# Expert products one stage deeper on 64x64 quarters, down weights fetched by number, and a reordered start of the second attention layer

## The chip, the core and the metric

The kernel runs on one core of one Trainium2 chip. A core has a matrix engine (PE, with its weight loads shown apart as PEld), a vector engine (DVE), an activation engine (ACT), a general engine (POOL, GpSimd), a queue engine that here only starts transfers (SP), and 16 DMA engines that carry the transfers of all of them. The metric is the device time of one run of the whole program, in microseconds (us). Everything is computed in float32 except a few counting steps.

## The reference, cut to what matters

Two layers over 1024 tokens (8 tiles of 128) with 256 channels. Each layer adds a mixing step and a feed-forward step to x, each behind a layer norm and scaled by tanh of a gate. The change touches the feed-forward step of layer 0 and the mixing step of layer 1.

```python
# layer 0: x += tanh(g) * wkv(ln(x), ctx)     a decaying scan
# layer 0, feed-forward: 64 experts, 4 chosen for each token, plus shared experts
logits = flat @ router_w
scores = softmax(logits)
_, topk_idx = top_k(logits + router_bias, 4)
topk_scores = take_along_axis(scores, topk_idx); topk_scores /= topk_scores.sum()
g = silu(einsum('nd,edf->nef', flat, wg))       # wg, wu: 64 x 256 x 64
u = einsum('nd,edf->nef', flat, wu)
routed = einsum('ne,nef,efd->nd', comb, g * u, wd)   # wd: 64 x 64 x 256
# layer 1: x += tanh(g) * attention(ln(x), ctx)   16 heads of 16; a query tile sees the 128 keys of its own row
# layer 1, feed-forward on block-quantised (fp8-like) weights and activations
```

The kernel does not compute all 64 experts for all tokens. It sorts the (token, expert) picks into blocks of 64 rows that share an expert and computes each block with its expert's weights alone.

## The kernel before

**Blocks and pairs.** There are room for 128 blocks of S = 64 rows. Two blocks (j = 0, 1) stand side by side in the 128 rows of a group, two groups (b = 0, 1) make a pair, so a pair is 4 blocks and 256 rows, and there are NP = 32 pairs. In the first NPS = 16 pairs block i belongs to expert i, known when the program is built. The blocks of the last 16 pairs take the overflow; their experts are found at run time and stand in the row `eid_row`, from which an engine loads them into registers (`experts_of`, a TENSOR_LOAD and one register operation for each use).

**The work on one pair** n passes through all engines:

- POOL gathers the rows of the pair from DRAM into one of four buffers `xg` (L519, two indirect transfers), up to three pairs ahead.
- PE transposes them (helper L1118, 4 transposes, semaphore `xgT_ps`), ACT copies them from PSUM into `xgT` (L700).
- PE multiplies with the up weights (`wg` and `wu` of the expert side by side). In the first 16 pairs (L1263) a block's product has 64 columns of weights' output rows, so the two blocks j use two 64-wide halves of the array; in the last 16 (L1270) the product is 128x128 and the rows that belong to the other block are zero. Semaphore `gu`.
- ACT takes the silu of the gate half (L694, `sgb`), DVE multiplies it with the other half (L1003, `hb`).
- PE transposes `hb` (L1118, 2 transposes, `hT_ps`), ACT copies it into `hbT` (L705).
- PE multiplies with the down weights `moe_dn`, which hold all 64 experts in partitions 0 to 63 of `arena_dn`: 64 rows by 64 outputs for the first 16 pairs (L1291), 64 rows by 128 outputs, accumulated over j with the other block's columns zero, for the last 16 (L1294). Semaphore `mo_y`.
- ACT copies the result into `ysb` (L711, two buffers), SP stores it to `ys_dram` (L395), 256 KB a pair, semaphores `ys_out0` and `ys_out1`.

Each float32 product or transposed product shows as two passes in the trace where it has a separate weight load for each (16 records for the 8 up products of a pair, 8 for the 4 down products).

**The order on the engines** is written out by hand, as one step k of a loop per engine. PE's step k: up products of pair k, transposes of pair k+1, down products of pair k-1, transposes of `hb` of pair k. ACT's step k: silu k, `xgT` k+1, `hbT` k, `ysb` k-1. DVE's step: `hb` k, and then halves of the quantising of a weight matrix for the last stage (`weight_half`, 48 halves in all, 4 instructions each, L989 to L997); how many have been done after step n is told by `weight_halves(n)`. POOL finishes each weight (L511, `weight_rescale`) between its gathers.

**The end of the loop.** SP waits for the last up products, then starts six loads of keys and values of attention (`kva_load`, L384 and L385, 256 KB each, tiles 0 to 2), and then the last store L395. POOL, which has to wait for all stores, then gathers each token's four expert results (`gather`, L543, four indirect transfers a tile) for DVE to add (L1016, `combine`). PE in that time transposes the quantised weights (`mx_turns`, out of `mx_w`).

**The start of the attention.** For a tile: layer norm (DVE L1069 and L1071 statistics, POOL L444 and L447 inverse root, DVE L1049 `xnE`), transposes, ACT copy L744, query projection L1347, bias L1021 on DVE, square on ACT L740, inverse root on POOL L552 (`query_rms`), norm on DVE L1026, transposes, copy L1033 to `qT`, scores L1333, DVE maximum L1043 over them, then the transposed scores L1380, exponentials on ACT (L753), and the product with the values L1341. POOL's layer-norm step for tile 1 stands behind all four gathers of tile 2; PE computes the scores of tile 0 in its step k = 1.

## Time and profile before

| | us |
|---|---|
| median of the three runs | 546.87 |
| lowest, highest | 544.39, 546.98 |
| the profiled execution | 548.21 |
| its span, first to last instruction | 546.5 |
| mean granted clock of TensorE, share of full | 0.863 |
| PE busy | 419.4 (77%) |
| DVE busy | 355.8 (65%) |
| POOL busy | 240.2 (44%) |
| ACT busy | 161.9 (30%) |

The profile is of one execution. Its page sums up busy time by engine, and cuts the span into 40 equal slices with a digit in tenths for each engine, for the granted clock (PEclk) and for the DMA engines. The chain of work that ended last is followed back from the last instruction, at each step to what released it. The timeline lists instructions with start, length and, in brackets, the idle time ahead of them and who ended it. Ends of matmuls are modelled, so the start of whoever waits for a product is the safer sign of when it was ready. The expert loop runs from 182 us to 309 us, the attention layer from 309 us to about 420 us, the last feed-forward stage from there to the end.

### The profile page before, as it was taken

The numbers are of one execution on the slowest core, as the hardware profiler recorded it, in microseconds if no ns is written. First come the engines' busy times: TensorE is split into PE (matmuls) and PEld (weight loads), VectorE is DVE, ScalarE is ACT, GpSimd is POOL, SyncE is SP. The second block draws the span as 40 slices with busy tenths as digits, with TensorE's granted clock in tenths as the row PEclk, the third lists the DMA queues.
The fourth block names the chain that finished last, engine by engine and source line by source line (L and its number), as shares of the span: only waits on it lengthen the run. The fifth ranks groups of instructions, "written<-read, shape, count | busy, mean of one in ns | idle before, by whom it ended". The sixth has DMA issues, their size and how long they took to land.

```text
span 546.5 us, 8075 instructions
## 1 busy us (share of the span) xinstructions
PE 419.4 (77%) x2711; PEld 287.4 (53%) x2711; DVE 355.8 (65%) x898; ACT 161.9 (30%) x374; POOL 240.2 (44%) x336
## 2 busy tenths in 40 slices
PE   0777653389685699999999934788988599999885
PEld 0565532234264465578888623566665245555543
DVE  3658889993644014567877425577851599999992
ACT  1444520123100155543333430344442122222210
POOL 2355533323203667766561156756200345555451
PEclk9999855579869599999999875599995599999997
DMA  7126999900055656554652422243200000000000
GB/s 213 35 71 214 284 276 220 231 14 1 1 118 153 229 163 173 163 148 102 124 113 80 150 83 68 69 133 100 79 1 1 1 1 11 10 11 10 10 10 20
DMA packets 66968, 53.19 MB, mean 97 GB/s; under 512 B 37872, under 2 KB 59504, under 8 KB 66928
## 3 DMA queue, kind: packets, MB, share of 16 engines
q1 hardware_dynamic: 56688, 34.09, 24.4%
q0 software_dynamic: 4608, 12.59, 9.5%
q10 hardware_dynamic: 5632, 6.00, 3.2%
q8 instruction: 23, 0.38, 0.3%
q14 instruction: 17, 0.14, 0.1%
HBM read 37.98 MB, written 14.68 MB: 96 GB/s over the span
## 4 chain that ended last, share of the span: by engine, by line
PE 44%; DVE 23%; issue 15%; POOL 10%; ACT 4%; DMA 4%; another core or an unknown queue 0%; POOLq 0%; SPq 0%; DVEq 0%; ACTq 0%
PE psum L1118 8%; PE psum L1212 5%; PE psum L1270 5%; PE psum L1294 5%; PE psum L1263 5%; POOL arena_dn L588 3%; PE psum L1235 3%; POOL mx_w L591 2%; DVE arena_dn L828 2%; PE psum L1380 2%; PE psum L1333 2%; PE psum L1386 2%; DMA x_res<-in_x_dram 1%; DVE arena_dn L935 1%; POOL arena_up L543 1%
## 5 line engine op out<-in xcount | busy, mean ns | idle before, releaser
L519 POOL DMA_INDIRECT shared<-h_dram,tok_u x64 | 63.9, 998 | 60.0 <-PE psum L1235 28.0
L1407 PE MATMUL psum<-arena_dn 128*128 128x512 f32 x128 | 59.7, 621 | 3.7 <-ACT arena_dn L762 3.7
L1118 PE MATMUL psum<-ident,arena_dn 128*128 128x128 f32 x112 | 23.2, 334 | 49.0 <-DVE arena_dn L858 15.0
L1118 PEld LDWEIGHTS psum<-ident,arena_dn 128*128 128x128 f32 x112 | 15.5, 169 | 56.1 <-issue 23.3
L1407 PEld LDWEIGHTS psum<-arena_dn 128*128 128x128 f32 x128 | 24.6, 198 | 34.2 <-issue 28.4
L1003 DVE TENSOR_TENSOR h1T<-psum,h1T 128x128 f32<-128x128 f32 x32 | 9.3, 291 | 50.4 <-ACT h1T L694 41.8
L588 POOL TENSOR_TENSOR arena_dn<-arena_dn 128x512 f32<-128x512 f32 x16 | 20.3, 1270 | 45.7 <-DVE arena_dn L974 45.7
L1118 PE MATMUL psum<-ident,arena_up 128*128 128x128 f32 x128 | 23.6, 312 | 21.5 <-DVE arena_up L1049 13.5
L543 POOL DMA_INDIRECT arena_up<-ys_dram,slot_u x32 | 31.5, 985 | 16.3 <-issue 16.3
L1118 PE MATMUL psum<-ident,mx_w 128*128 128x128 f32 x128 | 23.4, 320 | 12.7 <-POOL mx_w L591 9.6
L1294 PE MATMUL psum<-arena_dn,h1T 64*128 x128 | 31.9, 389 | 0.5 <-ACT h1T L705 0.5
L1118 PEld LDWEIGHTS psum<-ident,arena_up 128*128 128x128 f32 x128 | 16.1, 156 | 30.1 <-issue 9.8
L1423 PE MATMUL psum<-arena_dn,mx_w 128*128 128x256 f32 x128 | 30.7, 395 | 0.1
L1212 PE MATMUL psum<-h1T,shared 128*128 128x512 f32 x64 | 29.7, 623 | 0.0
L1118 PE MATMUL psum<-ident,shared 128*128 128x128 f32 x128 | 21.5, 294 | 9.3 <-DMA shared<-h_dram,tok_u 9.3
L1118 PEld LDWEIGHTS psum<-ident,mx_w 128*128 128x128 f32 x128 | 16.5, 161 | 22.5 <-POOL mx_w L591 11.7
L1423 PEld LDWEIGHTS psum<-arena_dn,mx_w 128*128 128x128 f32 x128 | 25.0, 200 | 3.7 <-ACT mx_w L773 0.4
L1294 PEld LDWEIGHTS psum<-arena_dn,h1T 64*128 64x128 f32 x128 | 22.7, 186 | 6.0 <-issue 3.1
L1016 DVE SCALAR_TENSOR_TENSOR x_res<-arena_up,combs,x_res 128x256 f32<-128x256 f32 x32 | 15.4, 481 | 15.2 <-DMA arena_up<-ys_dram,slot_u 14.6
L444 POOL TENSOR_SCALAR small<-mv 128x1 f32<-128x1 f32 (+2 forms) x26 | 6.4, 246 | 41.9 <-DVE mv L1085 20.0
L1043 DVE TENSOR_REDUCE arena_up<-psum 128x16 f32<-128x2048 f32 x8 | 18.3, 2293 | 7.7 <-PE psum L1333 5.9
L511 POOL TENSOR_TENSOR mx_w<-mx_w,wac 128x256 f32<-128x256 f32 x24 | 14.8, 620 | 19.1 <-DVE mx_w L997 18.3
(215 smaller groups left out, 993.0 us busy)
## 6 DMA issues: line engine op xcount, KB each, us to landing
ys_dram<-ysb SPq DMA_DIRECT2D x32, 256.0 KB
arena_up<-in_L_ffn_wg_dram SPq DMA_DIRECT2D x8, 512.0 KB, 7.5
arena_up<-in_L_ffn_wu_dram SPq DMA_DIRECT2D x8, 512.0 KB, 8.3
arena_dn<-in_L_ffn_wd_dram SPq DMA_DIRECT2D x4, 1024.0 KB, 11.6
va_dram<-mx_w ACTq DMA_DIRECT2D x8, 256.0 KB, 4.4
kT_dram<-mx_w ACTq DMA_DIRECT2D x8, 256.0 KB, 4.4
arena_up<-kT_dram SPq DMA_DIRECT2D x8, 256.0 KB, 2.7
arena_up<-va_dram SPq DMA_DIRECT2D x8, 256.0 KB, 3.0
```

The costliest lines, as they stand in the source:

```text
L519: pool.indirect_dma_start(out=xg[n % 4][:, b, :], out_offset=None, in_=h1_dram[:, :], in_offset=bass.IndirectOffsetOnAxis(ap=tok_u[:, 2 * ...
L543: pool.indirect_dma_start(out=yk[n % 3][k], out_offset=None, in_=ys_dram[:, :], in_offset=bass.IndirectOffsetOnAxis(ap=slot_u[:, n * K + k ...
L588: pool.tensor_tensor(haF[h], haF[h], heF[h], ALU.subtract).then_inc(sem("hint"), 1)
L1043: dve.tensor_reduce(qn[b % 2].rearrange("p (g j) d -> p j g d", g=4)[:, :, :, HD], psum[:, 0:4, :].rearrange("p j (g n) -> p j g n", g=4), ...
L1118: return pe.transpose(dst, src, ident[0:k, 0:k])
L1212: ins = pe.matmul(bank[2 * part + n % 2][:, :], sgu_w[:, c, part * SH + f * P:part * SH + (f + 1) * P], h1T[:, c, hf * 512:(hf + 1) * 512] ...
L1235: ins = pe.matmul(bank[2 + t % 2][:, 0:D], hs[:, f, t * P:(t + 1) * P], sd_w[:, f, :], start=(f == 0), stop=(f == 3))
L1263: ins = pe.matmul(bank[2 + k % 2][at, 2 * F * b:2 * F * (b + 1)], xgT[k % 2][:, b, c, j, at], moe_up[:, c, Q * (2 * k + b) + j, :], start= ...
L1270: ins = pe.matmul(bank[2 + k % 2][:, 2 * F * b:2 * F * (b + 1)], xgT[k % 2][:, b, c, j, :], moe_up[:, c, experts[k][Q * b + j], :].rearran ...
L1294: ins = pe.matmul(bank[6 + n % 2][:, b * D:(b + 1) * D], hbT[n % 2][0:F, b, j, :], moe_dn[:, experts[n][Q * b + j], :].rearrange("p a d -> ...
L1407: ins = pe.matmul(bank[2 + 2 * part + h][:, :], xTF[s][:, c, :], mx_gu[:, c, lo:lo + HW], start=(c == 0), stop=(c == C - 1))
L1423: ins = pe.matmul(bank[1][:, 0:D], hTF[s][:, k, :], mx_dn[:, k, :], start=(k == 0), stop=(k == 7))
```

## The change

Five edits:

1. **One stage deeper.** PE's step k is now: up k, transposes k+1, down k-2, `hb` transposes k-1. ACT's step: silu k, `xgT` k+1, `ysb` k-2, `hbT` k-1. The loops have one step more.
2. **Down weights by number, on quarters.** In the last 16 pairs SP loads the four experts' down weights of a pair from DRAM into a new double buffer `dnS`, experts j = 0 into partitions 0 to 63 and j = 1 into partitions 64 to 127; `hbT` puts its block j = 1 into partitions 64 to 127 as well (two ACT copies where there was one); and each down product is 64 rows by 64 outputs, on the quarter of the array that belongs to its rows and outputs. Nothing in `hbT` has to be zero now, so DVE's two clearing instructions go.
3. **Weight halves.** Nine halves in four steps in the last 16 pairs, where it was seven in three.
4. **Last store first.** SP's last store goes ahead of the loads of keys and values.
5. **Tile 0's attention first.** The scores of tile 0 and their maximum move one step earlier, the transposes of tile 2's row and their copy move behind tile 0's transposed scores and exponentials, and POOL's four gathers of tile 2 are split around `query_rms(0)` and the layer-norm step of tile 1.

```diff
-    return min(min(max(n - 4, 0), NPS - 5) + 7 * max(n - NPS + 1, 0) // 3, 2 * NWC)
+    return min(min(max(n - 4, 0), NPS - 5) + 9 * max(n - NPS + 1, 0) // 4, 2 * NWC)
...
+            def dn_load(n):
+                s = n % 2
+                if n >= NPS + 2:
+                    sp.wait_ge(sem("mo_y"), n - 1)
+                for x, v in enumerate(experts_of(mybir.EngineType.SP, n)):
+                    b, j = x // Q, x % Q
+                    sp.dma_start(dnS[s][j * F:(j + 1) * F, b, :], wd[bass.ds(v, 1)].rearrange("a f d -> f (a d)"))\
+                      .then_inc(sem(f"dn_in{s}"), 16)
+
+            sp.wait_ge(sem("eid"), 1)
             for n in range(NP):
-                if n == NP - 1:
-                    sp.wait_ge(sem("gu"), NG // 2)
-                    for b in range(2):
-                        sp.wait_ge(sem(f"kva_out{b}"), 32 * (T // 2))
-                    for t in range(3):
-                        kva_load(t)
+                if NPS <= n + 2 < NP:
+                    dn_load(n + 2)
                 sp.wait_ge(sem("ysb"), n + 1)
                 sp.dma_start(ys_dram[n * 2 * P:(n + 1) * 2 * P, :].rearrange("(b p) d -> p b d", p=P),
                              ysb[n % 2][:, :, :]).then_inc(sem(f"ys_out{n % 2}"), 16)
-            for n in range(3, T):
+            sp.wait_ge(sem("gu"), NG // 2)
+            for b in range(2):
+                sp.wait_ge(sem(f"kva_out{b}"), 32 * (T // 2))
+            for n in range(T):
                 kva_load(n)
...
+            def down(n):
+                pe.wait_ge(sem("hbT"), n + 1)
+                if n >= NPS:
+                    pe.wait_ge(sem(f"dn_in{n % 2}"), 64 * ((n - NPS) // 2 + 1))
+                reach(pe, sem("ysb"), n - 1)
...
+                            ins = pe.matmul(bank[6 + n % 2][at, b * D:(b + 1) * D], hbT[n % 2][j * F:(j + 1) * F, b, at],
+                                            dnS[n % 2][j * F:(j + 1) * F, b, :], start=True, stop=True)
...
-                                ins = pe.matmul(bank[6 + n % 2][:, b * D:(b + 1) * D], hbT[n % 2][0:F, b, j, :],
-                                                moe_dn[:, experts[n][Q * b + j], :].rearrange("p a d -> p (a d)"),
-                                                start=(j == 0), stop=(j == Q - 1))
...
+                    if n < NPS:
+                        act.copy(hbT[n % 2][0:F], turned).then_inc(sem("hbT"), 1)
+                    else:
+                        act.copy(hbT[n % 2][0:F, :, 0:S], turned[:, :, 0:S])
+                        act.copy(hbT[n % 2][F:2 * F, :, S:P], turned[:, :, S:P]).then_inc(sem("hbT"), 1)
...
+            gather(0, range(K))
+            gather(1, (0, 1))
+            row_rms(0)
+            gather(1, (2, 3))
+            gather(2, (0,))
+            query_rms(0)
+            gather(2, (1,))
+            row_rms(1)
+            gather(2, (2, 3))
...
+                if k == 0:
+                    score_max(0)
```

On PE, in a step of the last 16 pairs, the instructions between the up products of one pair and those of the next stood before as follows (`shared` is the gathered row buffer, `h1T` holds `hb` and `hbT`, `arena_dn` the down weights):

```order
L1118 MATMUL psum<-ident,shared 128x128 [waits xgT,xg0]
L1118 MATMUL psum<-ident,shared 128x128 x3
L1294 ISA [waits ysb,hbT]
L1294 MATMUL psum<-arena_dn,h1T 128x256
...
L1118 MATMUL psum<-ident,h1T 64x128 [waits hbT,hb]
L1118 MATMUL psum<-ident,h1T 64x128
L1249 TENSOR_LOAD eid_row [waits hb,xgT]
```

and stand now, on PE in the same place, as follows (the helper for transposes is L1153 now, and `h1T` holds `dnS` too):

```order
L1153 MATMUL psum<-ident,shared 128x128 [waits xgT,xg2]
L1153 MATMUL psum<-ident,shared 128x128 x3
L1311 MATMUL psum<-h1T 64x256 [waits ysb,dn_in1,hbT]
L1311 MATMUL psum<-h1T 64x256 x3
L1153 MATMUL psum<-ident,h1T 64x128 [waits hbT,hb]
L1153 MATMUL psum<-ident,h1T 64x128
L330 TENSOR_LOAD eid_row [waits hb,xgT]
```

The places are the same, but the down products now have 64 outputs and no register operation, wait for the fetched weights, and belong to the pair before the one they belonged to; the transposes behind them do too.

On SP, at the end of the expert loop, the stores of results and the loads of keys and values stood before as follows:

```order
L395 DMA ys_dram<-ysb 128x2x256 [waits ysb] x31
L384 DMA arena_up<-kT_dram 128x512 [waits kva_out1,kva_out0,gu]
L385 DMA arena_up<-va_dram 128x512
...
L395 DMA ys_dram<-ysb 128x2x256 [waits ysb]
L384 DMA arena_up<-kT_dram 128x512 [waits pv]
```

and now, on SP from the last fetch of down weights on (one of the four transfers of a fetch is shown):

```order
L330 TENSOR_LOAD eid_row [waits mo_y]
L401 ISA
L401 DMA h1T<-in_L_ffn_wd_dram 64x256
...
L409 DMA ys_dram<-ysb 128x2x256 [waits ysb] x3
L392 DMA arena_up<-kT_dram 128x512 [waits kva_out1,kva_out0,gu]
L393 DMA arena_up<-va_dram 128x512
```

The last store no longer stands behind six loads, and ahead of 16 of the stores stands a register load and four transfers.

On POOL, at the start of the attention, the gathers (L543) and the inverse roots (L444 with L447, and L552) stood before as follows:

```order
L543 DMA arena_up<-ys_dram,slot_u 128x256 x2
L552 TENSOR_TENSOR arena_up<-arena_up,mhalf 128x1 [waits ssq]
L543 DMA arena_up<-ys_dram,slot_u 128x256 x4
L444 TENSOR_SCALAR small<-mv 128x1 [waits mvE]
L447 TENSOR_TENSOR rstd<-small,mhalf 128x1 [waits isq]
L563 TENSOR_TENSOR x_res<-x_res,bias_bc 128x256 [waits xnE]
```

and now, on POOL in the same place (L560 is the gather, L461 with L464 and L567 the roots):

```order
L560 DMA arena_up<-ys_dram,slot_u 128x256 x3
L567 TENSOR_TENSOR arena_up<-arena_up,mhalf 128x1 [waits ssq]
L560 DMA arena_up<-ys_dram,slot_u 128x256
L461 TENSOR_SCALAR small<-mv 128x1 [waits mvE]
L464 TENSOR_TENSOR rstd<-small,mhalf 128x1 [waits isq]
L560 DMA arena_up<-ys_dram,slot_u 128x256 x2
L585 TENSOR_TENSOR x_res<-x_res,bias_bc 128x256 [waits xnE]
```

One gather of tile 2 moved ahead of the query's root, and the layer-norm root of tile 1 moved ahead of two.

## Rows read from the trace of the kernel before

**Rows 1.** Windows: busy us of PE, PEld, DVE, ACT, POOL; clock, DMA share, GB/s.

```profile
244.00:298.00 54.00, 54.00 (x364) 45.94 (x363) 42.55 (x126) 20.58 (x50) 27.08 (x34) 1.00 0.49 107
321.00:357.00 36.00, 18.85 (x158) 13.48 (x158) 19.28 (x36) 6.31 (x12) 25.05 (x32) 0.50 0.25 74
```

**Rows 2.** Timeline, weight loads of one late step: start us, us, engine, line, operation.

```profile
261.47 1.86 PEld L1270 LDWEIGHTS psum<-arena_up,shared 128*128 128x128 f32 x16
...
263.89 1.59 PEld L1294 LDWEIGHTS psum<-arena_dn,h1T 64*128 64x128 f32 x8 [0.17 <-issue]
...
265.81 0.14 PEld L1118 LDWEIGHTS psum<-ident,h1T 128*64 128x64 f32 x2 [0.33 <-issue]
...
265.95 1.86 PEld L1270 LDWEIGHTS psum<-arena_up,xgT 128*128 128x128 f32 x16
```

**Rows 3.** Timeline, weight loads of pairs 16 and 17, and of pair 31.

```profile
235.40 1.86 PEld L1270 LDWEIGHTS psum<-arena_up,shared 128*128 128x128 f32 x16 [0.66 <-issue]
...
237.82 0.62 PEld L1291 LDWEIGHTS psum<-arena_dn,h1T 64*64 64x64 f32 x8 [0.17 <-issue]
238.83 0.14 PEld L1118 LDWEIGHTS psum<-ident,h1T 128*64 128x64 f32 x2 [0.39 <-issue]
239.06 1.86 PEld L1270 LDWEIGHTS psum<-arena_up,xgT 128*128 128x128 f32 x16
...
301.82 1.87 PEld L1270 LDWEIGHTS psum<-arena_up,xgT 128*128 128x128 f32 x16
```

**Rows 4.** Timeline, one early step: up products, silu, next up products.

```profile
228.61 0.85 PEld L1263 LDWEIGHTS psum<-arena_up,shared 128*64 128x64 f32 x16 [0.20 <-issue]
...
230.80 0.28 ACT L694 ACTIVATE h1T<-psum 128x128 f32<-128x128 f32 x1 [1.23 <-PE psum L1263]
...
231.85 0.85 PEld L1263 LDWEIGHTS psum<-arena_up,xgT 128*64 128x64 f32 x16 [0.20 <-issue]
```

**Rows 5.** Waits between 244 and 298 us: total us, times, longest.

```profile
DVE h1T L1003 <- ACT h1T L694: 8.2, 8, 1.3
```

**Rows 6.** One line's instructions: ns min/median/max; then an issue of SP's queue.

```profile
L1249 PEldq TENSOR_LOAD <-eid_row x16: 327/332/513, 234.7 to 300.5; - x16
...
L1270 PEldq FUSED_REGOPS  x128: 46/46/46, 235.3 to 301.9; - x128
...
309.95 0.43 SPq L385 DMA_DIRECT2D arena_up<-va_dram  x1
```

**Rows 7.** Page, DMA issues: KB each, median us from issue to landing.

```profile
kT_dram<-mx_w ACTq DMA_DIRECT2D x8, 256.0 KB, 4.4
arena_up<-kT_dram SPq DMA_DIRECT2D x8, 256.0 KB, 2.7
```

**Rows 8.** Chain that ended last: start us, us, what.

```profile
173.70 6.70 DMA shared<-h_dram,tok_u
...
307.12 2.14 DMA ys_dram<-ysb
309.27 7.70 issue
316.97 0.99 POOL arena_up L543
```

**Rows 9.** Timeline, the last copy of results and the last store.

```profile
308.70 0.59 ACT L711 COPY ysb<-psum 128x512 f32<-128x512 f32 x1 [1.60 <-PE psum L1294]
...
310.43 0.43 SPq L395 DMA_DIRECT2D ys_dram<-ysb  x1
```

**Rows 10.** Timeline, start of the attention: POOL's roots, DVE's statistics of tile 1.

```profile
331.19 0.71 POOL L552 TENSOR_TENSOR arena_up<-arena_up,mhalf 128x1 f32<-128x1 f32 x1 [2.48 <-ACT arena_up L740]
...
334.88 0.18 DVE L1071 BATCH_NORM_AGGREGATE mv<-stats 128x2 f32<-128x6 f32 x1
...
336.94 0.19 POOL L444 TENSOR_SCALAR small<-mv 128x1 f32<-128x1 f32 x1
...
343.96 0.19 POOL L444 TENSOR_SCALAR small<-mv 128x1 f32<-128x1 f32 x1
```

180 lines of the change are left out of this document (95 added, 85 removed).

## The prediction

> **What bounds the kernel now.** I read first the windows of the stages that the change touches, for busy time and clock, then the timeline of single steps, and last the chain of waits where two stages meet. In the late half of the expert loop (pairs 17 to 31) PE is never idle: 54.00 us busy of 54.00, at full clock [rows 1]. One step there lasts from one set of up products to the next, 261.47 to 265.95, 4.48 us [rows 2], and 14 such steps lie between 239.06 and 301.82 [rows 3], 62.76 / 14 = 4.48. The down products take 1.92 us of it, 263.89 to 265.81 [rows 2]. DVE is the second: it is busy 42.55 us and waits only 8.2 of the 54 [rows 1, 5]. In the early half the step is about 3.2 us, and it is a loop, not a full engine: up products to silu, silu to the copy of the next rows, copy to the next up products [rows 4]. Behind the loop POOL stands still for 7.70 us, 309.27 to 316.97, because the last store lands late [rows 8]. The attention then starts at half clock, 0.50 from 321 to 357 us, with PE busy half the time [rows 1], and is led by POOL and DVE.
>
> **The late half, on PE.** One step of before already has the new shape: in step 16 the up products are the wide ones of the late half and the down products are still those of pair 15, 64 by 64. It takes 239.06 - 235.40 = 3.66 us, and its down products take 238.83 - 237.82 = 1.01 us [rows 3] against 1.92 [rows 2]. So PE alone would give 4.48 - 3.66 = 0.82 us a step. The register load is in that row too and stays hidden.
>
> **The late half, on DVE.** Its work is (54 - 8.2) us in 54 / 4.48 = 12.05 steps, 3.80 us a step with the gaps between instructions [rows 1, 5]. About 0.33 of it is the product `hb`, the rest 7/3 halves of a weight. With 9/4 halves it is (3.80 - 0.33) x 2.25 / 2.333 + 0.33 = 3.68 us. So DVE is next, at the same height as PE. Being one stage deeper, PE needs `hb` of a pair only after the down products of the following step, some 5 us after its up products end (a step of 3.7, that step's transposes and 1.0 of down products), so an uneven share of 2 or 3 halves is smoothed and only DVE's mean counts. PE gives 3.66, DVE 3.68; for the jitter between them and more POOL traffic beside DVE I take 3.72, with 3.66 and 4.0 as ends. Gain: 14 x (4.48 - 3.72) = 10.7 us, ends 6.7 and 11.5.
>
> **SP and the fetched weights.** A fetch stands on SP between a wait for the down products of pair n and the store of pair n. The trace has no transfer whose address comes from a register; the nearest rows are a register load of 0.33 us and a register operation of 0.05 on PE, and plain issues 0.48 us apart on SP, 309.95 to 310.43 [rows 6, 9]. That makes 0.33 + 4 x (0.05 + 0.48) + 0.48 = 2.9 us a step for SP, less than 3.7, so SP has room. Queued behind the fetch is the store, so the store is issued about 2.5 us after the down products instead of 0.7. It must land before ACT reuses its buffer two steps (7.4 us) later: 2.5 + 0.5 + 4.4 (the landing of a store of this size on ACT's queue [rows 7]) = 7.4 at worst, 5.1 with the 2.14 us of [rows 8]. The weights must be there two steps after the fetch, less the products' own 1.0: 2.4 + 2.7 [rows 7] = 5.1 against 6.3. Both fit, the store barely; I take 0 for them and keep the rest for a rival. Traffic rises from 512 to 768 KB a step, from 107 [rows 1] to about 210 GB/s.
>
> **The early half.** Depth removes PE's wait for `hb` just ahead of the transposes. But the up products of the next pair must wait for `xgT`, which ACT copies only after the silu: the silu starts 2.19 us after the up products, and the next ones start 1.05 us behind it, time that goes to the silu, the copy and two hand-overs; 3.24 in all [rows 4]. This loop is not touched. I take 0.5 us for all the early steps, ends 0 and 3.5 (if the step fell by 0.3 in 11 of them). At pair 16 PE waits 0.66 us before the first wide products [rows 3], of which about 0.3 goes. One stage more puts one more set of down products, about 1.0 us, behind the last up products, and takes one set from between the first ones; with the longer row of copies at the end that is +0.1. ACT's second copy and DVE's two dropped clears lie beside PE's work and cost nothing while PE or DVE leads.
>
> **The last store.** The copy of the last results ends at 309.29, the store is issued at 310.43 behind six loads [rows 9], and lands at 316.97 [rows 8]: 7.68 us from copy to gather. The store of pair 30, with nothing ahead of it, landed in 2.14 us [rows 8]. With the new order: 0.1 + 2.14 to 3, gain 5.4 to 4.6; I take 5.2. What is late next is the first gather: the six loads (1.5 MB) now run beside it and not beside the store. Its landing may slip by up to 1 us; I take 0.3.
>
> **Tile 0's attention first.** POOL leads here. Before, its root for tile 1 came at 336.94, though the statistics were ready at 335.06, and its root for tile 2 at 343.96 [rows 10]. Now POOL does one gather inside the 2.48 us in which it waited for ACT, but then stands idle until 335.06 for tile 1. From one root to the other lay 7.0 us (root, addition, four gathers of tile 3); two gathers of tile 2 come in between now, 2 x 1.25 (0.99 [rows 8] and a gap): 335.1 + 7.0 + 2.5 = 344.6. That is 0.6 later than before, some of it given back where DVE's additions no longer run beside the gathers, and tile 1's bias waits behind it on DVE. Tile 0's scores come about 4.5 us earlier, but nothing that ends late hangs on them. I take +0.4, ends -2 (if tile 0's lead reaches the tiles behind) and +2 (if the clock, still 0.50 up to 357 [rows 1], rises later because PE's work lies more spread).
>
> **The sum.** Against the profiled execution's own 548.21: -10.7 - 0.5 - 0.3 + 0.1 - 5.2 + 0.3 + 0.4 = -15.9, 532.3. The median of the runs is 1.3 below that execution: 531.0. The ends together (each a little inside) give 524.5 and 537.
>
> **Rivals.**
>
> *The quarters do not run beside each other.* The two down products of a group use different rows of the array and write the same PSUM bank; no row of before has that (the 64 by 64 products of before share their rows). If they run one after another, each pass takes the 0.24 us of L1294, 8 passes make 1.92 again, the step stays 4.48, and only the store and small terms are left: 548.2 - 5.2 - 0.5 + 0.3 + 0.4 + 0.1 - 1.3 = 542.0. For it: the case has no row that excludes it. Against: their outputs lie in different partitions. The Trainium skill (TensorEngine Tiling (Array Packing), Gotcha 1: PSUM Pressure) says that different row tiles cannot access the same PSUM bank at one time; by that rule this rival is the result. The page does not say whether different output partitions of the bank are enough.
>
> *SP or POOL leads.* If a by-number issue costs over 0.72 us instead of 0.53, SP's step passes 3.7; at 0.85 it is 4.2. The store that lands late does the same through ACT, and POOL's wait for DVE's last half delays its gathers. Step 4.0 to 4.3: 14 x 0.4 us more, 535 to 539.
>
> *The fetched weights come late; slower than before.* Two steps cannot be shorter than fetch issue 2.4 + landing L + products 1.1. At L = 2.7 that is 3.1 us a step, harmless. It leads from L = 3.9, and the kernel is slower than before by the half per cent from L = 6.6: then the step is 5.05 and 15 of them lose 8.5, and the other terms give 5.6 of that back. A gather did take 6.70 us [rows 8], while the queues were full of weight loads. At that landing the time is about 550. Against it: the late half moves 107 GB/s now at a share of 0.49 [rows 1].
>
> **How the numbers follow.** Forecast (step 3.66 to 3.9) 0.60, 524.5 to 534.5. SP or POOL leads 0.17. Quarters one after another 0.11. Weights late 0.04, beyond 549.6. The rest, attention and clock off by more than 2 us either way, 0.08. The range 524 to 540 leaves out the quarters' case, the slow case and about 0.04 on the low side. Half a per cent, 2.7 us, is about what a measurement of this kernel can tell from no change: faster means under 544.1, which holds forecast, SP case and quarters case. Faster 0.91, same 0.04, slower 0.05.
>
> **What would show it.** In the trace of after: the down products of the late half 1.0 us long and the step 3.7; DVE without waits for ACT there; SP's fetch 2.5 us and done before the next down products; POOL's first gather about 2.4 us after the last copy; the early step still 3.1 to 3.2; the root for tile 2 as far behind the first gather as before (27.0 us). Wrong would be a late step over 4, a `dn_in` wait on PE, or an early step under 3.

## The result, and the profile after

The changed kernel takes 542.03 us (median of five runs, 540.89 to 542.29) against 546.87 us; the ratio is 0.9923, 95% interval 0.9901 to 0.9945. It is faster, but by 4.8 us where 15.9 were forecast, and 542.0 lies outside the range of 524 to 540. The profiled execution of after has a span of 540.3 us. Chips differ: on the five that ran the later kernels, the kernel before took 545.5, 540.0, 539.6, 539.6 and 546.8 us. So kernels of different chips are compared by their ratio to the kernel before on the same chip, and not by their microseconds; and since even the ratio of one kernel differs between a slower chip (545 to 547 us for the kernel before) and a faster one (540), best with a chip of the same speed. On the second of the 539.6 us chips the change gave only 0.9975 (0.9954 to 0.9997).

Three things of the forecast can be read at once. First, the late step. The timeline of TensorE's weight loads in the kernel after (start us, us, engine, line, operation):

```profile
244.33 1.86 PEld L1294 LDWEIGHTS psum<-arena_up,shared 128*128 128x128 f32 x16
246.11 0.47 PEld L1153 LDWEIGHTS psum<-ident,shared 128*128 128x128 f32 x4
246.75 0.62 PEld L1311 LDWEIGHTS psum<-h1T 64*64 64x64 f32 x8 [0.17 <-issue]
247.76 0.14 PEld L1153 LDWEIGHTS psum<-ident,h1T 128*64 128x64 f32 x2 [0.39 <-DVE h1T L1033]
247.96 1.86 PEld L1294 LDWEIGHTS psum<-arena_up,xgT 128*128 128x128 f32 x16
```

These answer to [rows 2, 3]. The down products on quarters take 247.76 - 246.75 = 1.01 us where they took 1.92, and a step is 247.96 - 244.33 = 3.63 us where it was 4.48. The quarters do run beside each other, and the step is a little shorter than the 3.72 of the forecast.

Second, that step doesn't last. Windows of the same stretches as [rows 1] (busy us of PE, PEld, DVE, ACT, POOL; clock, DMA share, GB/s), of after:

```profile
244.00:298.00 54.00, 48.37 (x370) 37.92 (x369) 43.63 (x125) 22.81 (x63) 28.22 (x34) 0.94 0.75 165
321.00:357.00 36.00, 20.83 (x174) 14.89 (x178) 20.52 (x40) 8.27 (x17) 22.20 (x29) 0.57 0.26 75
...
244.00:262.00 18.00, 18.00 (x152) 14.33 (x150) 16.73 (x47) 8.45 (x23) 12.06 (x15) 1.00 0.66 172
```

TensorE was busy in all 54.00 us before [rows 1]. Now it stands still for 5.6 of them, its mean granted clock is 0.94, and the transfer engines are busy for 0.75 of the time where they were for 0.49. Up to 262 us all is well: busy 18.00 of 18.00 at clock 1.00.

Third, the waits of after between 240 and 312 us (total us, times, longest), and the chain of work that ended last:

```profile
ACT ysb L728 <- DMA ys_dram<-ysb: 9.1, 3, 4.3
...
PEld psum L1311 <- issue: 8.3, 15, 2.8
```

```profile
277.60 0.30 SPq L330
278.04 0.23 issue
278.27 0.28 SPq L401
278.74 0.47 SPq L401
279.43 0.47 SPq L401
280.09 0.47 SPq L401
280.56 0.36 issue
280.92 10.26 DMA ys_dram<-ysb
```

L401 is the fetch of a late expert's down weights on SP, L409 the store of a pair's results, L728 ScalarE's copy of results into the store's buffer, L1311 the late down products. The second wait above is TensorE's ahead of late down products, up to 2.8 us long, ended by nothing that the profile names. A store of 256 KB needs 10.26 us here to land. ScalarE waits for such stores before it may write their buffer again, three times, and TensorE behind it. The timeline of ScalarE shows one of them; the wait stands in brackets:

```profile
284.72 0.59 ACT L728 COPY ysb<-psum 128x512 f32<-128x512 f32 x1 [4.33 <-DMA ys_dram<-ysb]
```

The forecast had 2.14 to 4.4 us for that landing, from [rows 7, 8].

The other place that matters is where the loop ends. POOL's timeline of after:

```profile
309.64 0.62 POOL L528 TENSOR_TENSOR mx_w<-mx_w,wac 128x256 f32<-128x256 f32 x1 [2.38 <-DMA ys_dram<-ysb]
313.68 1.00 POOL L560 DMA_INDIRECT arena_up<-ys_dram,slot_u  x1 [3.42 <-issue]
```

The last copy ends at 310.81, the first gather starts at 313.68: 2.87 us, where [rows 8, 9] had 7.68.

The steps as intervals between the copies of two pairs, from ScalarE's timeline (pair 18 to 19 first, pair 30 to 31 last). They are set here beside the three kernels on which most of what follows rests:

```
before            4.48 4.48 4.49 4.48 4.48 4.49 4.48 4.48 4.49 4.48 4.48 4.12 2.19
after             4.79 3.90 5.88 3.58 5.08 6.34 6.53 2.19 3.76 3.63 3.23 2.52 3.64
after_rows        3.67 3.64 3.72 3.64 3.78 3.64 3.67 4.14 3.19 3.64 3.24 4.29 3.90
one_fetch_rows    3.68 3.63 3.73 3.64 3.79 3.63 3.67 3.64 3.69 3.64 3.24 2.19 2.19
spread4_rows      3.63 3.64 3.63 3.64 3.63 3.63 3.64 3.63 3.63 3.64 3.20 2.19 2.18
```

The sum of the row of after is 55.1 us, that of the last row 43.9. So some 11.2 us are lost in 13 steps, about what the forecast missed by (11.0).

### The profile page after: what moved, and what is told of

It is laid out like the page before. It is cut to its first block, busy times and chain, and to the rows that moved or that the text cites. A ratio compares the mean times of both kernels' runs of the same rounds, so it can differ in the third digit from the quotient of the medians.

```text
span 540.3 us, 8236 instructions
## 1 busy us (share of the span) xinstructions
PE 405.7 (75%) x2711; PEld 273.3 (51%) x2711; DVE 355.9 (66%) x896; ACT 163.3 (30%) x390; POOL 239.5 (44%) x336
## 3 DMA queue, kind: packets, MB, share of 16 engines
q0 software_dynamic: 4608, 12.59, 10.4%
## 4 chain that ended last, share of the span: by engine, by line
PE 35%; issue 24%; DVE 21%; POOL 9%; ACT 4%; DMA 4%; SPq 1%; POOLq 0%; DVEq 0%; ACTq 0%
PE psum L1153 8%; PE psum L1247 6%; PE psum L1294 4%; PE psum L1285 3%; POOL arena_dn L610 3%; PE psum L1308 3%; POOL mx_w L613 2%; DVE arena_dn L860 2%; PE psum L1367 2%; PE psum L1311 2%; DMA ys_dram<-ysb 2%; DMA x_res<-in_x_dram 2%; PE psum L1424 2%; PE psum L1432 1%; PE psum L1453 1%
## 5 line engine op out<-in xcount | busy, mean ns | idle before, releaser
L1153 PE MATMUL psum<-ident,arena_dn 128*128 128x128 f32 x112 | 22.9, 331 | 51.5 <-DVE arena_dn L839 15.9
L1153 PEld LDWEIGHTS psum<-ident,arena_dn 128*128 128x128 f32 x112 | 15.1, 166 | 58.1 <-issue 24.0
L560 POOL DMA_INDIRECT arena_up<-ys_dram,slot_u x32 | 31.3, 977 | 11.3 <-issue 11.0
L1153 PE MATMUL psum<-ident,arena_up 128*128 128x128 f32 x128 | 23.0, 303 | 15.5 <-DVE arena_up L1056 5.0
L1153 PE MATMUL psum<-ident,mx_w 128*128 128x128 f32 x128 | 24.4, 333 | 12.5 <-POOL mx_w L613 9.6
L1247 PE MATMUL psum<-h1T,shared 128*128 128x512 f32 x64 | 30.9, 644 | 0.0
L1153 PE MATMUL psum<-ident,shared 128*128 128x128 f32 x128 | 22.0, 298 | 9.3 <-DMA shared<-h_dram,tok_u 9.3
L1153 PEld LDWEIGHTS psum<-ident,mx_w 128*128 128x128 f32 x128 | 17.4, 168 | 22.5 <-POOL mx_w L613 11.7
L1153 PEld LDWEIGHTS psum<-ident,arena_up 128*128 128x128 f32 x128 | 15.4, 151 | 23.6 <-DVE arena_up L1056 6.1
L461 POOL TENSOR_SCALAR small<-mv 128x1 f32<-128x1 f32 (+2 forms) x26 | 6.4, 247 | 43.1 <-DVE mv L1120 17.1
L728 ACT COPY ysb<-psum 128x512 f32<-128x512 f32 x32 | 18.9, 591 | 20.9 <-PE psum L1311 10.0
L1311 PE MATMUL psum<-h1T 64*64 64x256 f32 x128 | 18.3, 405 | 7.1 <-issue 5.3
L716 ACT ACTIVATE h1T<-psum 128x128 f32<-128x128 f32 x32 | 8.9, 278 | 45.4 <-PE psum L1285 22.5
## 6 DMA issues: line engine op xcount, KB each, us to landing
arena_dn<-in_L_ffn_wd_dram SPq DMA_DIRECT2D x4, 1024.0 KB, 11.4
```

Source lines behind the costliest of these rows:

```text
L560: pool.indirect_dma_start(out=yk[n % 3][k], out_offset=None, in_=ys_dram[:, :], in_offset=bass.IndirectOffsetOnAxis(ap=slot_u[:, n * K + k ...
L728: act.copy(ysb[n % 2][:, :, :], bank[6 + n % 2][:, :].rearrange("p (b d) -> p b d", b=2))\
L1153: return pe.transpose(dst, src, ident[0:k, 0:k])
L1247: ins = pe.matmul(bank[2 * part + n % 2][:, :], sgu_w[:, c, part * SH + f * P:part * SH + (f + 1) * P], h1T[:, c, hf * 512:(hf + 1) * 512] ...
L1311: ins = pe.matmul(bank[6 + n % 2][at, b * D:(b + 1) * D], hbT[n % 2][j * F:(j + 1) * F, b, at], dnS[n % 2][j * F:(j + 1) * F, b, :], start ...
```

## Experiments

Where a ratio is given it is to the kernel before, measured on the same chip together with it, with its 95% interval. The expectations are in microseconds of the chip of the result, where the kernel before takes 546.9 and the changed kernel 542.0. The first theory (A) was that the fetches cost this, by their place on SP (A1) or by their bytes (A2).

### First group: take the fetch away, move it, halve it, spread it

**no_fetch** leaves out all fetches but the first two pairs'.

```
-                if NPS <= n + 2 < NP:
+                if NPS <= n + 2 < NPS + 2:
```

> Leaves out 14 of the 16 late fetches: pairs 18 to 31 reuse the weights that pairs 16 and 17 fetched, so the second half's outputs are other numbers. Theory A (the fetches, by their place on SP or by their bytes, make the stalls): the late steps stay at the 3.64 us that pairs 19 to 23 of the changed kernel show, no ScalarE wait for a store and none at the silu of 263 us; 15 steps at 3.64 from 240.87 put the last copy at about 302, some 8.5 us earlier, so 533 to 535 us. Rival B (the stalls come from instruction loading or the clock and would be there without fetches): 540 to 542. Rival C (the queue is busy with gathers and stores alone): stores still wait, 538 to 541.

532.83 us, 0.9743 (0.9691 to 0.9794). No store wait; steps of 3.59 to 3.73 with one of 4.18, and 3.20, 2.19, 2.19 at the end. Without the fetches the gain that was forecast is there (531.0 to 546.87 is 0.971).

**store_first** puts the two blocks on SP the other way round.

```
             for n in range(NP):
-                if NPS <= n + 2 < NP:
-                    dn_load(n + 2)
                 sp.wait_ge(sem("ysb"), n + 1)
                 sp.dma_start(ys_dram[n * 2 * P:(n + 1) * 2 * P, :].rearrange("(b p) d -> p b d", p=P),
                              ysb[n % 2][:, :, :]).then_inc(sem(f"ys_out{n % 2}"), 16)
+                if NPS <= n + 2 < NP:
+                    dn_load(n + 2)
```

> On SP each pair's store goes ahead of the fetch that stood before it; the same transfers and bytes. Theory A1 (order on SP: the store is issued 2.4 to 3 us late, behind four by-number fetches): stores land 2.4 us earlier, the three ScalarE waits of 9.1 us together shrink to under 3, 536 to 538 us. Rival A2 (bytes: fetch 256 KB, store 256 KB and gather 256 KB in 3.64 us are more than the queues carry): the waits stay or move to TensorE's wait for fetched weights, since the fetch is now what comes late, 540 to 544.

548.34 us, 1.0042 (1.0009 to 1.0075), slower than before. The wait of ScalarE for a store is gone, and in its place TensorE waits before the down products, which the trace calls issue (240 to 312 us):

```profile
PEld psum L1311 <- issue: 13.0, 14, 2.7
...
PE psum L1311 <- issue: 10.3, 9, 2.5
```

**half_bytes** fetches 32 KB an expert for 64.

```
-                    sp.dma_start(dnS[s][j * F:(j + 1) * F, b, :], wd[bass.ds(v, 1)].rearrange("a f d -> f (a d)"))\
+                    sp.dma_start(dnS[s][j * F:(j + 1) * F, b, 0:D // 2],
+                                 wd[bass.ds(v, 1), :, 0:D // 2].rearrange("a f d -> f (a d)"))\
```

> Each fetch brings only half of its columns (32 KB for 64 KB, in as many transfers, by number as before); the other half of the tile keeps what was there, so half of the late columns are other numbers. Theory A2 (bytes): the load falls from 768 to 640 KB a step and the store waits of 9.1 us go down to under 3, 535 to 537 us. Rival A1 (time and order on SP): 542 as the changed kernel, within 1.5.

543.44 us, 0.995 (0.9929 to 0.997). With half the bytes nothing is won that can be told from the changed kernel's 0.9923. Theory A2 in its simple form falls.

**spread4** gives every late pair's weights a place of their own, fetches them from ahead of the loop on, two transfers a step behind the store, and has four store buffers for two (not shown in the cut).

```
+        dnE = arena_dn[:, 0:NPS * 2 * D].rearrange("p (n b d) -> p n b d", n=NPS, b=2)
+            early = [(m, 1) for m in range(4)]
+            later = [(m, j) for m in range(NPS) for j in range(2) if (m, j) not in early]
...
             for n in range(NP):
...
+                if n < len(later):
+                    dn_load(*later[n])
```

> All late weights get a place of their own (the columns that early pairs are done with, and the partitions beside them), fetched two transfers a step from before the loop on behind each pair's store, and the store buffers go from two to four. Theory A (either form): no store wait, no late weights, late steps 3.64 from pair 18 to 31, the last copy some 8 us earlier than in the changed kernel; early steps stay near 3.0 if 128 KB more a step is hidden: 532 to 535 us. Rival: the fetches disturb the early half instead (its gathers and stores), 537 to 541.

535.73 us, 0.9815 (0.9766 to 0.9864), a version better than the changed kernel. It still has one step of 5.65 and one of 4.19 us, and its early steps were 3.1 to 3.7 us, where those of the other kernels on that chip were 3.0 to 3.3.

### Second group: SP's time against bytes

In the trace of after SP goes round in 3.63 us (251.98 to 255.61), in step with TensorE, and its own work fills nearly all of it: from the load of the numbers (0.30) to the end of the fourth fetch 2.91 us, the store 0.58, and the gaps beside it 0.1, 3.59 in all. SP's timeline, after:

```profile
251.98 2.43 SPq L401 DMA_DIRECT2D h1T<-in_L_ffn_wd_dram  x4
254.46 0.58 SPq L409 DMA_DIRECT2D ys_dram<-ysb  x1
255.61 2.43 SPq L401 DMA_DIRECT2D h1T<-in_L_ffn_wd_dram  x4
```

From the load of the numbers to the end of the fourth fetch, chain of after (276.22 - 273.30):

```profile
273.30 0.30 SPq L330
...
275.75 0.47 SPq L401
```

That made theory S: SP has no slack against TensorE's 3.64, so a delay is never made good.

**one_fetch** brings the same bytes in one transfer from a fixed place.

```
-                for x, v in enumerate(experts_of(mybir.EngineType.SP, n)):
-                    b, j = x // Q, x % Q
-                    sp.dma_start(dnS[s][j * F:(j + 1) * F, b, :], wd[bass.ds(v, 1)].rearrange("a f d -> f (a d)"))\
-                      .then_inc(sem(f"dn_in{s}"), 16)
+                m = 4 * (n - NPS)
+                sp.dma_start(dnS[s], wd[m:m + 4].rearrange("(b j) f d -> (j f) b d", b=2))\
+                  .then_inc(sem(f"dn_in{s}"), 16)
```

> The same 256 KB a pair, but as one transfer of four neighbouring experts at a fixed place: one issue on SP for four, and no register loads. The down projection of the second half uses experts by place and not by number, so its outputs are other numbers. Theory S (SP's time: in the changed kernel's trace fetch 2.43, store 0.58 and the loads of the numbers 0.5 make 3.58 us of the 3.64 us step, so a delay is never made good): SP has 2.4 us a step free, no store wait, late steps 3.64, last copy near 301.5: 533 to 535 us. Rival B (bytes and their place in one queue with the stores): 540 to 543 as the changed kernel.

**tiny_fetch** keeps four transfers by number, of one row each.

```
-                    sp.dma_start(dnS[s][j * F:(j + 1) * F, b, :], wd[bass.ds(v, 1)].rearrange("a f d -> f (a d)"))\
+                    sp.dma_start(dnS[s][j * F:j * F + 1, b, :], wd[bass.ds(v, 1), 0:1, :].rearrange("a f d -> f (a d)"))\
```

> Four transfers by number a pair as in the changed kernel, but one row of 1 KB each: SP does all its issuing and nearly no bytes move. All but one row of each late down tile is what was there before. Theory S (SP's time): SP's cycle stays near 3.5 us and the stalls stay: 540 to 543 us. Rival B (bytes, or landing): no waits, 533 to 535. Between them, 536 to 539, if an issue of few rows takes SP less than the 0.47 us of one of 64 rows, which the trace will show.

**four_stores** has four store buffers for two.

```
+        dnS = [arena_dn[:, 2 * D * i:2 * D * (i + 1)].rearrange("p (b d) -> p b d", b=2) for i in range(2)]
+        ysb = [sb(f"ysb{i}", [P, 2, D]) for i in range(2)] + [take(2, D) for _ in range(2)]
```

> Four store buffers for two (the fetched tiles move to the columns of experts 0 to 3, free by then); order, transfers and bytes as in the changed kernel. If the ScalarE wait for a store to land (9.1 us in three) is what costs, and not what follows it, the time falls to 534 to 536 us. Theory S expects less: SP still runs at 3.58 us a step without slack, and a late fetch makes TensorE wait in place of the late store, 537 to 541.

**spread2** is spread4 with two store buffers.

> As the version with the fetches spread over 28 steps, two transfers each behind the store, but with two store buffers as in the changed kernel. Theory S: SP is free for over half of each step, stores are issued at once, 534 to 537 us, within 1.5 of the version with four buffers. Rival (slow landing of stores whatever SP does): 538 to 541.

one_fetch: 533.77 us, 0.9893 (0.9858 to 0.9928). tiny_fetch: 530.95 us, 0.985 (0.9804 to 0.9897). four_stores: 537.99 us, 0.9957 (0.9932 to 0.9983). spread2: 534.22 us, 0.9899 (0.9829 to 0.997).

All four ran on a chip where the kernel before takes 540.0, so the microseconds of the expectations don't apply as they stand. Set against the 0.9975 that the changed kernel later gave on a chip of this speed, one_fetch wins 4.4 us, tiny_fetch 6.8, four_stores 1.0 and spread2 4.1, where theory S had expected 7 to 9 of one_fetch. None fits theory S alone. The issue of four one-row fetches took SP only 1.50 us, so tiny_fetch doesn't isolate SP's time as meant. one_fetch frees SP, and still has steps of 5.44, 5.74, 5.55 and 4.54 us; spread2 has 6.51 and 8.14, with a store wait of up to 6.35 us, though SP had time to spare. All these stalls lie between 262 and 292 us. Since the single transfer of one_fetch has landings that the trace resolves, it could be read there. DMA issues of one_fetch (KB each, median us from issue to landing), first in 236 to 252, then in 268 to 284 us:

```profile
h1T<-in_L_ffn_wd_dram SPq DMA_DIRECT2D x4, 256.0 KB, 3.8
shared<-h_dram,tok_u POOLq DMA_INDIRECT x8, 4.0
```

```profile
h1T<-in_L_ffn_wd_dram SPq DMA_DIRECT2D x3, 256.0 KB, 9.5
...
shared<-h_dram,tok_u POOLq DMA_INDIRECT x4, 9.6
```

The same transfer needs 3.8 us and then 9.5, and the gather of token rows on POOL's queue 4.0 and then 9.6. So something slows all transfers from some 262 us on. The share of the software queue (q0, the gathers; packets, MB, share of 16 engines' time) shows what. Share times window over MB is the price of one MB. Of before in 190 to 236 and in 262 to 274 us:

```profile
q0 software_dynamic: 1351, 3.70, 30.7%
```

```profile
q0 software_dynamic: 286, 0.78, 46.5%
```

One MB costs 0.307 x 46 / 3.70 = 3.8 us of all 16 engines in the first stretch and 0.465 x 12 / 0.78 = 7.2 us in the second. The slow stretch was there before the change; with a step of 4.48 us nothing waited for it. The token table holds 0 in every slot that has no token. The second half's blocks are for what runs over the first 64 tokens of an expert, so late pairs are mostly or wholly empty, and the gather of an empty group of two blocks reads row 0 of h1_dram 128 times over. That is theory H: a hot row.

### Third group: the hot row

```
-            dve.tensor_copy(tok_u[:, :], bank[5][:, 0:NG]).then_inc(sem("tok"), 1)
+            chain(dve.tensor_scalar(prod[:, 0, :], bank[5][:, 0:NG], 0.0, pcol[:, 0:1], ALU.is_equal, ALU.mult), "r")
+            dve.scalar_tensor_tensor(tok_u[:, :], bank[5][:, 0:NG], -1.0, prod[:, 0, :], ALU.add, ALU.max)\
+                .then_inc(sem("tok"), 1)
```

The table now counts tokens from 1; a slot left at 0 takes its own partition's number as row. after_rows is the changed kernel with this edit, before_rows the kernel before with it, spread4_rows is spread4 with it, and old_attention the changed kernel with the old start of the attention and without it.

> The changed kernel, but the empty slots of the token table fetch 128 different rows of h1_dram in place of row 0 all of them (two small VectorE operations more; the outputs are the same, since no token reads an empty slot). Theory H (one hot row: from about 252 us on the software queue's packets take 8 to 10 us of 16 engines' time per MB where they took 4.2 before 236 us, and everything else that moves through those engines lands late): the share of that queue in 262 to 274 us falls from 53% to about 27%, no store wait, late steps 3.64: 532 to 535 us. Rival S (SP's time, 3.58 us of a 3.64 us step): stalls stay, 540 to 543.

> The same edit alone on the kernel before, whose late steps are 4.48 us, set by TensorE and VectorE, with no wait for a transfer in them. Theory H and its rivals alike: no change within 0.3%, though the software queue's share in 252 to 274 us should fall from 46% to about 25%.

> The changed kernel with the start of the attention (tile 0's order on TensorE, VectorE, ScalarE and GpSimd, and the early gathers of tile 2) as before. In the changed kernels of this study the time from the first gather of expert outputs to the end is 224 to 228 us, before it was 229.5. Theory: the order is worth those 3 us, so this one takes 3 us more than the changed kernel, 544 to 546. The prediction's step gave it a cost of 0.4, so 541 to 542 us. The time from the first gather to the end tells it apart from the stalls before it.

> Late weights fetched from the first step on, two transfers a step behind the store, four store buffers, and the empty slots' rows spread: all late steps at 3.64 us and no wait for a transfer from 190 us on. 530 to 533 us; by theory H no better than the changed kernel with spread rows by more than 2 us, by rival S better than it by 6 to 9.

**after_rows**: 530.56 us, 0.9823 (0.9789 to 0.9857). **before_rows**: 540.02 us, 1.0004 (0.9978 to 1.003). The software queue in 262 to 274 us, of after and then of after_rows:

```profile
q0 software_dynamic: 274, 0.77, 53.0%
```

```profile
q0 software_dynamic: 349, 0.97, 29.7%
```

One MB takes 0.297 x 12 / 0.97 = 3.7 us of 16 engines in after_rows, where after has 0.530 x 12 / 0.77 = 8.3. The store waits are down from 9.1 us to 0.9, and the steps are those of the table above. The expected 532 to 535 us are 7 to 10 under the changed kernel; on chips of this speed it is 8.2 (see after_again below). The same edit gives nothing to the kernel before, as all theories had it: there nobody waited for a transfer.

**spread4_rows**: 526.45 us, 0.9748 (0.9709 to 0.9788), the best kernel of this study, 1.8% under the changed kernel by the ratio 0.9923 and 2.3% under it on this kind of chip. Every late step is 3.63 or 3.64 us from pair 18 until the loop runs out (3.20, 2.19, 2.18). Theory H had it within 2 us of after_rows, rival S 6 to 9 better; by the ratios it is 0.0075 x 540 = 4.1 us better, between the two. So SP's time is a second, smaller cause.

**old_attention**: 537.11 us, 0.9945 (0.9918 to 0.9972), no difference that can be told, neither from 0.9923 nor from the 0.9975 (0.9954 to 0.9997) of the changed kernel on a chip of this speed. From the first gather to the end its trace has 226.0 us, as the kernels with the new order.

### Fourth group: SP's share, the dose, the last store

> The changed kernel with spread rows for empty slots, and the late weights as one transfer a pair at a fixed place (the second half uses experts by place, so its outputs are other numbers): the same bytes as the changed kernel, 0.6 us of SP in place of 2.9 a pair. If SP's time is what remains, the last two steps fall from 4.29 and 3.90 to 2.19 and no step from pair 19 on is over 3.7: 4 to 4.5 us under the changed kernel with spread rows (ratio 0.974 to before, near 526). If the bytes are what remains, the same as it, 0.982.

> The changed kernel with every slot's token set to 0, so that all rows of all gathers of the expert loop are row 0 (the expert outputs are other numbers, the work is the same). By the hot row theory the software queue needs 8 to 10 us of 16 engines per MB from the first step on, where the changed kernel needs 4.2 in 190 to 236 us, so gathers or stores come late in the first half too: steps over 3.2 us there, 550 us or more in all. If the slow stretch was due to something else at that time in the program, no change: 540 to 543.

```
-            dve.tensor_copy(tok_u[:, :], bank[5][:, 0:NG]).then_inc(sem("tok"), 1)
+            dve.tensor_scalar(tok_u[:, :], bank[5][:, 0:NG], 0.0, None, ALU.mult).then_inc(sem("tok"), 1)
```

> The kernel before with its last store ahead of the k and v loads, nothing else. Theory (the term of -5.2 us, seen as -4.8 in the trace from the last copy to the first gather): 4 to 5 us faster, ratio 0.991 to 0.993, which is about all of what the whole change gave. Rival (the loads beside the gathers, and what comes after, give it back): ratio 0.996 to 1.000.

```
-                if n == NP - 1:
-                    sp.wait_ge(sem("gu"), NG // 2)
-                    for b in range(2):
-                        sp.wait_ge(sem(f"kva_out{b}"), 32 * (T // 2))
-                    for t in range(3):
-                        kva_load(t)
...
-            for n in range(3, T):
+            sp.wait_ge(sem("gu"), NG // 2)
+            for b in range(2):
+                sp.wait_ge(sem(f"kva_out{b}"), 32 * (T // 2))
+            for n in range(T):
                 kva_load(n)
```

> The changed kernel itself, for its ratio on this chip beside the others: 0.992 as measured, within 0.003.

**one_row**: 565.57 us, 1.042 (1.0374 to 1.0467). With one row read by all gathers the kernel takes 0.0445 x 540 = 24 us more than the changed kernel on the same chip. The first half now stalls too, with steps up to 9.38 us. The software queue of one_row in 190 to 236 us:

```profile
q0 software_dynamic: 1199, 3.26, 76.9%
```

That is 0.769 x 46 / 3.26 = 10.9 us of 16 engines for one MB, against 0.349 x 46 / 3.80 = 4.2 in the changed kernel at that place. It isn't the time in the program that slows the gathers, it is the row.

**after_again**: 537.98 us, 0.9975 (0.9954 to 0.9997), against 0.9823 for the same kernel with spread rows on a chip of the same speed: the hot row costs the change 0.0152 x 540 = 8.2 us. On the slower chips it is less: 0.9923 against the 0.9822 of the fifth group, 0.0101 x 547 = 5.5 us. And in the late steps it costs little without the fetches. In no_fetch the row is as hot in 262 to 274 us, 0.676 x 12 / 0.79 = 10.3 us of 16 engines for one MB, and its steps hold but for one of 4.18:

```profile
q0 software_dynamic: 284, 0.79, 67.6%
```

**one_fetch_rows**: 528.24 us, 0.9783 (0.9757 to 0.9809). The last two steps fall from 4.29 and 3.90 to 2.19 as SP's theory has it, and no step before them is over 3.8 (3.7 was expected). Where TensorE stood in after_rows and no longer does, timeline of its weight loads, first after_rows, then one_fetch_rows:

```profile
292.38 0.14 PEld L1155 LDWEIGHTS psum<-ident,h1T 128*64 128x64 f32 x2 [0.39 <-DVE h1T L1035]
295.08 0.85 PEld L1313 LDWEIGHTS psum<-h1T 64*64 64x64 f32 x8 [2.56 <-issue]
```

```profile
293.24 0.14 PEld L1154 LDWEIGHTS psum<-ident,h1T 128*64 128x64 f32 x2 [0.39 <-DVE h1T L1034]
294.41 0.63 PEld L1312 LDWEIGHTS psum<-h1T 64*64 64x64 f32 x8 [1.04 <-ACT h1T L738]
```

In the traces the steps from pair 18 on make 48.2 us in after_rows and 43.9 in spread4_rows, and 3.8 of the difference of 4.3 lies in the last two. By the ratios one_fetch_rows wins 0.004 x 540 = 2.2 us, half of what I had expected, with intervals that overlap, so that this pair alone doesn't tell the 2.2 from nothing. With spread4_rows beside it, 2 to 4 us is SP's share once the rows are spread. The loop from its first up products to its last copy takes 112.5 us in one_fetch_rows and 112.3 in spread4_rows, against 122.8 in before_rows: -10.3 and -10.5, where the forecast had -11.4. With both causes away the forecast of the loop holds to within 1.1 us.

**before_store**: 534.87 us, 0.9924 (0.9894 to 0.9954). One edit of five, the last store ahead of the loads, gives the kernel before 4.1 us, as much as the whole change gave in the first measurement (0.9923) and more than it gave on this chip (0.9975).

### Fifth group: the order of the attention

> The changed kernel with the empty slots' rows spread, and the start of the attention (tile 0's order, the early gathers of tile 2) as before. By the prediction's step (+0.4 us for the new order) this is 0.4 us faster than the changed kernel with spread rows, the same within what a run can tell; if the new order pays, it is 2 us or more slower.

> The changed kernel with the empty slots' rows spread once more, beside the one with the old attention order: ratio 0.982 to the kernel before, as measured.

On a chip where the kernel before took 546.8 us: rows_old_attn 537.08 us, 0.9823 (0.9799 to 0.9847); after_rows_again 536.78 us, 0.9822 (0.9793 to 0.9851). The new order of tile 0 is worth nothing that these runs can tell, either way. On this chip the early steps are 3.1 us where the faster ones have 2.96, and after_rows_again still has five late steps of 4.1 to 5.1 us, with TensorE's wait for late weights (8.5 us over 18 times):

```profile
PEld psum L1313 <- issue: 8.5, 18, 3.0
```

Its ratio is that of the faster chip all the same, 0.9822 and 0.9823. In the microseconds of the result it would be 0.9822 x 546.87 = 537.1 us, still 6 over the forecast of 531.0: in its trace the loop takes 305.09 - 183.43 = 121.7 us, where the forecast had 126.9 - 11.4 = 115.5.

## Why the prediction was wrong, point by point

- **The late half on PE and DVE** (3.66 and 3.68, taken as 3.72): right. 3.63 us measured up to 262 us, and DVE no longer the limit.
- **The quarters' rival**: fell. The Trainium skill (TensorEngine Tiling (Array Packing), Gotcha 1: PSUM Pressure) has it that different row tiles cannot access one PSUM bank at a time. The eight down products here use two row tiles and write one bank, in different output partitions, and take 1.01 us, as the ones that share their rows did [rows 3]. Here the measurement decides against the rule as it is worded. That the measured 542.03 is the 542.0 of this rival is chance.
- **SP and the fetched weights** ("Both fit, the store barely; I take 0"): this is the step that failed, in both of its halves. The landing was taken as 2.14 to 4.4 us from [rows 7, 8], rows from other stages; in the late half a store took up to 10.26 us. What it lacked was the price of a transfer in this very stretch, which the trace of before could have given: its software queue costs 3.8 us of 16 engines for one MB in 190 to 236 us and 7.2 in 262 to 274. I read the mean share of 0.49 in 244 to 298 as room, and it was two stretches with different limits. That term is 8.2 us on the faster chips (after_again against after_rows) and 5.5 on the slower ones, of which the measured chip is one. And SP's time was put at 2.9 us a step, from an issue of 0.48 and a register operation of 0.05; its own work measured 3.59, of which 2.43 is the four fetches, about 0.6 each, and 0.58 the store. So SP had next to nothing to spare against 3.64, and that term is 2 to 4 us. The two don't simply add: taking SP's issues away alone won 4.4 us (one_fetch), spreading the rows alone 8.2, both together (0.9975 - 0.9783) x 540 = 10.4.
- **SP or POOL leads** (535 to 539 us, 0.17): the rival that was nearest. It named both ways, an issue that is dearer and a store that lands late through ACT, and sized them at 0.4 us a step; the late steps lost 11.2 us in 13, 0.9 a step.
- **Weights late; slower than before** (0.04): a kernel of this kind exists, and it is store_first, 1.0042, where the fetch stands behind the store.
- **The early half** (-0.5) and pair 16 (-0.3): the early steps are 2.96 us on the faster chips in kernels of either kind, and 3.0 to 3.3 on the others. The depth gives them nothing that shows. The wait ahead of the first wide products, 0.66 us before [rows 3], didn't shrink but is 1.14 in the timeline of after:

```profile
237.03 1.86 PEld L1294 LDWEIGHTS psum<-arena_up,shared 128*128 128x128 f32 x16 [1.14 <-issue]
```

- **The end of the loop** (+0.1): missed with SP's time. The last steps are 2.52 and 3.64 in after, where 2.19 each is what they take when the weights are there.
- **The last store** (-5.2): right. 7.68 to 2.87 us in the trace is -4.8, and -4.1 as a kernel of its own.
- **The attention** (+0.3 and +0.4): nothing measurable. The root for tile 2 comes 342.02 - 313.68 = 28.3 us after the first gather (27.0 before), 1.3 for the two together where 0.7 was forecast; but it is 27.0 again in after_again, and the fifth group shows no difference from the order. The profiled kernel before needed 229.5 us from its first gather to the end, after 226.6; before_rows and before_store, which lack the new order too, needed 224.7 and 225.4, and after_again 223.8. So nothing shows that this difference is the change's.
- **What the sum didn't hold**: the loop started at 185.40 and not at 182.35. The sixteen profiled executions of kernels with the change start it at 183.4 to 185.9 us (one_row, at 187.0, aside), the three without at 181.9 to 183.4; the two sets touch, so a shift of up to 3 us in a pair is not all shown to be the change's. In the profiled pairs it is there from the first loads on. The chain of before, before_store, then of after, after_again:

```profile
2.27 7.89 DMA x_res<-in_x_dram
```

```profile
2.27 7.37 DMA x_res<-in_x_dram
```

```profile
2.28 9.85 DMA x_res<-in_x_dram
```

```profile
2.28 9.98 DMA x_res<-in_x_dram
```

  The load of tiles 2 to 7 (768 KB) lands 2 to 2.6 us later, though nothing near it in the program was changed; the one of the first two tiles (256 KB) lands after 3.2 to 3.5 us in all four. Over all runs the large load takes 7.4 to 8.5 us in the three kernels without the change and 8.4 to 10.3 in those with it, on different chips. I haven't found the cause; that the longer program is being loaded beside it is a guess that no run here tests.

Together, in the profiled executions: the start of the loop +3.05, the loop -1.5 where -11.4 was forecast, last copy to first gather -4.8, first gather to the root of tile 2 +1.35, the rest -4.3 (which nothing shows to be the change's): -6.2 of 546.5.

Open besides the late start: one silu at 263.20 us in after waited 2.25 us, and the next up products with it, for something the trace puts to no engine; and why the slower chip keeps stalls of up to 5 us with the rows spread.

## What to carry to other kernels

Before a stretch is shortened, read the price of one MB on each queue in that very stretch, not the mean share of the stage: a queue that is slow for its own reasons is harmless until the step comes down to it. Padding that points every empty slot at one row of DRAM is not free: here it slowed the gathers themselves and the fetches and stores beside them. Spreading it over 128 rows cost two small operations; it was worth 1.0 to 1.5% in the changed kernel, and nothing in the kernel before, where nobody waited for a transfer (1.0004). Count each by-number transfer at what its engine needs for it, and compare the sum with the new step, not with the old one.

## What the runs showed of the hardware that I had not expected

- Gathers that all read one row of 1 KB take 10.9 us of 16 engines' time for one MB, those of many rows 3.3 to 4.2 (one_row; before_rows in 262 to 274 us and the changed kernel in 190 to 236), and a 256 KB transfer of another queue beside the hot row of the late pairs lands in 9.5 us for 3.8 (one_fetch). Why one row is slow, no run here shows.
- A fetch of 64 rows at an address from registers took SP about 0.6 us with its register work (2.43 for four), one of a single row 0.37 (1.50 for four).
- 64 by 64 products with different row tiles and different output partitions of one PSUM bank ran at 1.01 us for eight passes, where eight of 64 by 128 took 1.92 [rows 2].
- Such stalls cost once more by TensorE's clock: after a wait of 1.86 us the same 16 up products took 2.78 us, and 1.84 where no wait stood ahead of them. The granted clock is 1.00 in 262 to 264 us, 0.92 in 264 to 266, 0.50 in 266 to 268 and 1.00 again in 294 to 302. The chain of after:

```profile
262.71 1.86 issue
264.57 2.78 PE psum L1294 x16
...
297.49 1.84 PE psum L1294 x16
```
